# Attention phase of a macaron block: router logits and place counts between the denominators' matmuls

## What is computed

```
x = x + 0.5 * ffn(layernorm(x))
x = x + attn(layernorm(x))
x = x + 0.5 * ffn(layernorm(x))
```

```
Q = phi(x @ Wq); K = phi(x @ Wk); V = x @ Wv        # phi(x) = elu(x) + 1
num = Q . cumsum(K V);  den = max(Q . cumsum(K), 1e-6)
out = (num / den) @ Wo
```

## Time and profile before

| what | value |
|---|---|
| median of three runs | 1948.5 us (1945.95 to 1950.04) |
| the profiled execution's own time | 1945.28 us |
| its span, first to last instruction | 1943.5 us |
| TensorE matmuls busy | 1683.9 us, 87% |
| weight loads busy | 1373.8 us, 71% |
| VectorE busy | 1575.3 us, 81% |
| ScalarE busy | 1074.5 us, 55% |
| GpSimd busy | 968.9 us, 50% |
| mean granted TensorE clock | 0.962 of 2.4 GHz |

### The profile page before, as it was taken

One profiled execution on the slowest core, in us unless ns is written; L12 is line 12 of the kernel. 1 busy time (PEld: TensorE's weight loads), 2 busy tenths in 40 slices (PEclk: granted clock), 3 DMA queues, 4 the chain that ended last, 5 costly groups with the idle time before them and its releaser, 6 DMA issues. The chain is left out here.

```text
span 1943.5 us, 36383 instructions
## 1 busy us (share of the span) xinstructions
PE 1683.9 (87%) x12527; PEld 1373.8 (71%) x12527; DVE 1575.3 (81%) x4342; ACT 1074.5 (55%) x1935; POOL 968.9 (50%) x1010
## 2 busy tenths in 40 slices
PE   4449999956999999999999999999999966999990
PEld 3337778845787788778777878777877855777770
DVE  7769987746888899989899889988998726888884
ACT  2227677744546556565565555655656524777770
POOL 4777510116453465556546546546554323766661
PEclk9999999987999999999999999999999967999995
DMA  6675677720000010001001001001000004777758
GB/s 217 195 247 177 241 262 254 268 96 14 10 12 7 9 21 18 12 18 20 11 17 22 14 13 23 18 9 21 18 12 13 13 11 151 241 236 243 241 178 271
DMA packets 90512, 188.15 MB, mean 97 GB/s; under 512 B 14893, under 2 KB 52442, under 8 KB 79322
## 3 DMA queue, kind: packets, MB, share of 16 engines
q1 hardware_dynamic: 43434, 126.93, 19.5%
q0 software_dynamic: 33840, 46.17, 8.9%
q10 hardware_dynamic: 13056, 12.72, 1.9%
HBM read 131.08 MB, written 54.69 MB: 96 GB/s over the span
## 5 line engine op out<-in xcount | busy, mean ns | idle before, releaser
L1600 POOL TENSOR_TENSOR at_sc<-at_sc 128x512 f32<-128x512 f32 x128 | 198.6, 1551 | 318.7 <-DVE at_sc L1700 318.4
L565 ACT ACTIVATE f_hid<-f_up_ps,f_w 128x512 f32<-128x512 f32 x312 | 215.0, 689 | 140.4 <-PE f_up_ps L429 132.0
L1692 DVE SCALAR_TENSOR_TENSOR at_qk<-at_exps,at_relus 128x512 f32<-128x512 f32 x256 | 182.6, 714 | 89.7 <-ACT at_relus L1509 88.1
L1700 DVE TENSOR_TENSOR at_sc<-at_s_ps,mask 128x384 f32<-128x384 f32 x512 | 251.4, 548 | 1.1 <-PE at_s_ps L1333 1.1
L934 DVE TENSOR_TENSOR f_hid_lo<-f_hid,f_hid_hi 128x512 fp32r<-128x512 f32 x312 | 209.4, 689 | 14.9 <-ACT f_hid_hi L572 4.4
L2007 POOL DMA_INDIRECT x<-finished_rows,slot x120 | 195.7, 1631 | 29.6 <-issue 29.6
L685 POOL DMA_INDIRECT expert_rows<-f_rows_out,f_dest x156 | 167.6, 1074 | 78.7 <-DVE f_rows_out L962 40.3
L1573 ACT ACTIVATE raw<-at_num_ps 128x512 f32<-128x512 f32 x128 | 76.4, 597 | 220.0 <-PE at_num_ps L1370 220.0
L668 POOL DMA_INDIRECT sent_rows<-f_xn,slot x144 | 147.3, 1023 | 63.2 <-issue 42.0
L1330 PE MATMUL at_s_ps<-at_qk 64*128 64x256 f32 x1024 | 171.0, 411 | 7.3 <-issue 5.6
L1508 ACT ACTIVATE at_exps<-at_proj_ps 128x512 f32<-128x512 f32 x253 | 152.4, 602 | 34.7 <-PE at_proj_ps L1308 27.7
(11 more groups left out here) (338 smaller groups left out, 4745.1 us busy)
## 6 DMA issues: line engine op xcount, KB each, us to landing
f_w<-split_weights SPq DMA_DIRECT2D x78, 1028.0 KB, 5.3
f_got<-sent_rows SPq DMA_DIRECT2D x78, 264.0 KB, 5.0
finished_rows<-f_rows_out POOLq DMA_DIRECT2D x39, 256.0 KB, 2.8
split_weights<-f_split SPq DMA_DIRECT2D x8, 1024.0 KB, 4.9
sent_rows<-f_pads ACTq DMA_DIRECT2D x16, 264.0 KB, 7.6
x<-in_L_attn_x SPq DMA_DIRECT2D x16, 256.0 KB, 5.8
raw<-in_L_ffn_we SPq DMA_DIRECT2D x16, 256.0 KB, 6.3
out_x<-x ACTq DMA_DIRECT2D x16, 256.0 KB, 4.3
```

The source lines that it names most:

```text
L565: A(hid[:, c, :], up_bank(n)[:, :], ACT.Silu, bias=w[:, i % RING_W, 4 * HID + c:4 * HID + c + 1].bitcast(FP32)).then_inc(s_silu, 1)
L1600: g.tensor_tensor(sc[:, n % RING_SC, :, 3, :], sc[:, n % RING_SC, :, 1, :], sc[:, n % RING_SC, :, 2, :], ALU.add).then_inc(s_sum, 1)
L1692: stt(full, exps[:, p % 2, :], 1.0, relus[:, p % 2, :], ALU.min, ALU.add).then_inc(s_phi, 1)
L1700: last = tt(flat(sc[:, (n // 2) % RING_SC, 2 * (n % 2) + half, 0:3, :]), s_ps[2 * (n % 2) + half][:, 0:3 * P], flat(mask[:, :, :]), ALU.mult)
```

## The change

The logits and the place counts leave their place ahead of the denominators and stand among them. Of the four groups of four denominator matmuls (one group for each unit), the first is followed by one logits matmul, the second by the other, and the third by the five matmuls of the place count, where the step has them. For that the matmuls of logits and places no longer start an accumulation of their own (`start=False`): the first denominator matmuls do so for the bank. All waits of the three parts now stand ahead of the first denominator matmul. `has_sums` becomes `has_rest(s)`, which is true in the same steps as before (1 to 32). No matmul is added or removed.

```diff
-            def logits():
-                for q in range(BQ):
-                    last = mm(logit_ps[:, q * E:(q + 1) * E], r1[:, q * P:(q + 1) * P], rw2_half[:, :], start=True, stop=True)
-                return last
+            def logits(q):
+
+                return mm(logit_ps[:, q * E:(q + 1) * E], r1[:, q * P:(q + 1) * P], rw2_half[:, :], start=False, stop=True,
+                          skip_group_check=True)
...
-            def denominators(s):
+            def denominators(s, r, t):
+
 
                 pe.wait_ge(s_sum, UNITS * (s + 1))
                 for u in range(UNITS):
                     for j in range(4):
                         last = mm(num_ps[32 * j:32 * j + 32, 0:BT], den_sel[:, u, :], sc[:, (UNITS * s + u) % RING_SC, j, 0:4:3, :],
                                   start=(u == 0), stop=(u == UNITS - 1))
+                    if u < BQ and r is not None:
+                        logits(u)
+                    if u == BQ and t is not None:
+                        count_places(t)
                 return last
...
                         if has_logits(s):
                             pe.wait_ge(s_half, 2)
                             pe.wait_ge(s_r1, s - 3)
-                            last = logits()
                         if placed_in(s) is not None:
                             pe.wait_ge(s_route, 6 * placed_in(s) + 5)
-                            last = count_places(placed_in(s))
-                        if has_rest(s):
-                            last = denominators(s - 1)
+                        last = denominators(s - 1, s - 4 if has_logits(s) else None, placed_in(s))
                         last.then_inc(s_quad, 1)
```

More of the change, by code:

```diff
@@ L1212, in has_sums @@
         def has_sums(s):
-            return 1 <= s and (has_rest(s) or has_logits(s) or placed_in(s) is not None)
+            return has_rest(s)
         def ends_routed(s):
@@ L1339, in router_hidden @@
                 mm(slot_ps[:, 0:BT], k.rw1_lo[:, :], xT_hi[:, :], start=False, stop=True).then_inc(s_slot, 1)
-            def logits():
-                for q in range(BQ):
-                    last = mm(logit_ps[:, q * E:(q + 1) * E], r1[:, q * P:(q + 1) * P], rw2_half[:, :], start=True, stop=True)
-                return last
+            def logits(q):
+                return mm(logit_ps[:, q * E:(q + 1) * E], r1[:, q * P:(q + 1) * P], rw2_half[:, :], start=False, stop=True,
+                          skip_group_check=True)
             def count_places(t):
                 b = t % 2
-                mm(place_ps[:, :], k.before[:, :], flat(takes[:, b, :, :]), start=True, stop=False)
+                mm(place_ps[:, :], k.before[:, :], flat(takes[:, b, :, :]), start=False, stop=False, skip_group_check=True)
                 for q in range(1, TQ):
@@ L1353, in count_places @@
                 return mm(place_ps[:, :], k.every[:, :], k.so_far[:, b, :].unsqueeze(1).broadcast_to([P, TQ, E]),
-                          start=False, stop=True)
+                          start=False, stop=True, skip_group_check=True)
             def values(g):
```

## The result

The changed kernel takes 1962.4 us (median of three runs, 1960.7 to 1966.4) against 1948.5 us. The ratio is 1.0066, with a 95% interval from 1.0044 to 1.0088: slower by 13.9 us between the medians (1.0071 by them), where the prediction put 14.3 (1962.8 us). That the two are 0.4 us apart is partly luck, since the three runs spread by 4 us before and 6 us after.

What follows compares the result with a forecast made beforehand. It took a step to be a loop through TensorE, ScalarE and VectorE, TensorE's block time included; 15 x 0.37 + 13 x 0.65 + 0.3 = 14.3 us on 1948.5 gave 1962.8 us, range 1955.5 to 1966.5.

Steps and rivals of the forecast that it cites:

- The price of an insertion: In the denominator block, one logits insertion takes 0.33 + 0.14 + 0.18 + 0.24 = 0.89 us where two rounds took 0.43.
- The place insertion: Place-count matmuls among the denominators add 0.41 us, against 0.13 removed ahead of them: +0.28 us.
- the open bf16 load: First weight load of the inserted place matmuls, no longer loaded beforehand: 0.07 us, between bounds of 0 and 0.11.
- The counts: 15 steps with logits alone at 0.37 us, 13 with both at 0.65, step 32 with places alone at 0.3.
- It reaches the end: The block's whole 14.3 us passes to the kernel's time, since VectorE is held by the delay in even and odd steps.
- VectorE's idle time hangs on TensorE: VectorE idles 1.14 us, 6 us after the block, for a relu whose chain starts behind the block on TensorE.
- The odd-step rival: Odd steps swallow their delay through 0.3 us of VectorE slack: only 8.8 us slower, 1957.3 us; chance 0.06 to 0.08 class, given as 0.08.
- The small matmuls hide: Rival: whole-array weights load while column-group rounds stream, so insertions cost little; 7.3 us faster, 1941.2 us; chance 0.06.
- It costs more: Rival: each of 70 insertions pays a further 0.1 us, as with open second loads; 1969.8 us; chance 0.06.
- the first round's 0.24: First denominator round after entering the column groups takes 0.24 us instead of 0.217.

Runs made afterwards that it cites:

- five orders of the same matmuls: Same whole-array matmuls, only order differing; block with both: kernel before 2.54, changed 3.14, all behind 2.54, logits alone among 3.00, places alone among 2.77 us.
- the first chip: Place of the first comparison, unchanged kernel before against the changed kernel: 1948.5 and 1962.4 us, ratio 1.0066.
- the other chips: Chips of the experiment groups, where the changed kernel was run again against the kernel before: ratio 1.0035.
- split logits: Each logits matmul made four, one per 32-column group: among denominators in the changed kernel, 2016.9 us; ahead of them in the kernel before, ratio 1.0037.

## Why the prediction was right, point by point

- **The price of an insertion.** Each term was read where it already happened, and the sum, 0.89 us, is what the changed kernel shows twice in each block. From the start of the last denominator round to the logits it is 0.33 us (990.36 to 990.69), as the prediction said it should be. That the change of the array's division costs it was argued from step 32 and from pitches across waits. The count of changes shows it, 0.11 to 0.12 us for each in five orders of the same matmuls, and that is the 0.11 which the prediction read on the way out.
- **The place insertion** was mis-sized: the open bf16 load, for which I took 0.07 between bounds of 0 and 0.11, is worth 0.01 to 0.02 us, so 0.36 in place of 0.41. In 14 steps that is 0.7 us of the forecast's 14.3.
- **The counts.** 15 steps took 0.37 and 13 took 0.60 us more. In step 32, where 0.3 was forecast, the block went from 2.29 to 2.56 us, and there the agreement is luck: the kernel before run again has 2.67 us in it.
- **It reaches the end.** 97% on the first chip, with TensorE's waits for VectorE unchanged. The step that this rested on, that VectorE's idle time hangs on TensorE, held there: the 0.37 us of an odd step, for which VectorE was not ready at its read, arrived all the same (4.2 of 4.4 us). The odd-step rival was not wrong in kind: on the other chips most of the odd steps' share is swallowed, and the distance grew by the 8.8 us that it gave. Its reason was another, though (relus that are not the tie), where here something that the profile doesn't name holds VectorE. So the right time rests in part on where the first comparison ran.
- **The small matmuls hide** was wrong inside the block too: all 56 logits insertions have the same gap. The Trainium skill (TensorEngine Tiling (Array Packing), Key Properties) states that a change of the tiling mode drains TensorE, and the trace agrees, with 0.23 us for the pair of changes around one logits matmul. The same section says that different tiles can load weights and multiply in parallel, and in groups the same product cost 0.06 us.
- **It costs more** was wrong as well: the loads behind an insertion are not in the open beyond the first round's 0.24.

## What to carry to other kernels

Before a short matmul is tucked among others, look at which division of the array each uses, and count the changes: here each way out and back cost 0.23 us, and the product itself 0.22 on the whole array where it needs 0.06 in the neighbours' own division. If it must stand there, write it in that division, even as four times as many instructions. If it can stand at a place where the division changes anyway, one added change is all it pays, as the places did ahead of the split logits. And read the price of such a seam where the trace already has one, from start to start, and then ask which engine's idle time depends on the engine that got slower.

## What the runs showed that I had not expected

- **The same kernel ran 55 us slower in the experiments than in the first comparison.** Of the 65.5 us between the two profiled executions of the kernel before, 21.6 lie between step 4 and step 31. In the first one no engine stalls beside GpSimd's sends. On the three chips of the experiments ScalarE idled 1.5 us in each pair of steps (16.6 us in 11 times from 600 to 1500 us in the kernel before), VectorE 0.74 us, and steps from the first place count on took 35.9 us where they took 34.7 and 35.4. That it is the chips that differ fits this, but is not shown.
- **A dense run of short matmuls stalls beside the sends.** On those chips 36 records in the block ran at pace next to them, and 48, in the kernels with split logits, took 2 us longer. With the sends moved away the block is at pace again, so the stall comes with them. What the sends take from TensorE (its supply of instructions, a port, something else) is open. So is whether it is the number of records, their shortness or the column groups that makes the difference, and whether split logits alone would gain on the first chip, where this was not run.
- **A label is not a stall.** With the sends at their new place 11 us of TensorE's idle time ahead of L1256 changed from `at_an` to "issue", at 0.97 us each, as long as before. Idle time is to be compared with the same place of the other kernel before it is called new.
